# Key-value sums by pairs of tokens in a linear-attention and mixture-of-experts block

## The reference

```
kv = kv + outer(k_t, v_t)          # an 8 x 8 state, from zero in each sequence
ks = ks + k_t
num = q_t @ kv ;  den = q_t . ks + 1e-6
out_t = num / den                  # then out @ W_out + b_out
```

## Time and profile before

| | |
|---|---|
| median of 3 runs | 409.97 us (406.25 to 412.97) |
| the profiled execution | 410.09 us, its span 408.3 us |
| PE busy | 348.2 us, 85% of the span |
| DVE busy | 285.7 us, 70% |
| ACT busy | 264.1 us, 65% |
| POOL busy | 258.4 us, 63% |
| the 32 key-value scans on DVE | 72.9 us |
| the 512 output matmul passes L1302 on PE | 62.8 us |

### The profile page before, as it was taken

One profiled execution on the slowest core, in us unless ns is written; L12 is line 12 of the kernel. 1 busy time (PEld: TensorE's weight loads), 2 busy tenths in 40 slices (PEclk: granted clock), 3 DMA queues, 4 the chain that ended last, 5 costly groups with the idle time before them and its releaser, 6 DMA issues.

```text
span 408.3 us, 8196 instructions
## 1 busy us (share of the span) xinstructions
PE 348.2 (85%) x2523; PEld 299.0 (73%) x2530; DVE 285.7 (70%) x685; ACT 264.1 (65%) x700; POOL 258.4 (63%) x328
## 2 busy tenths in 40 slices
PE   7888498989878999888998839499999998998884
PEld 3447257887766878766787839389989998998863
DVE  4989488998978889987944504176554538777666
ACT  4959266796976859786536733256655558678665
POOL 8786675657849587593885556466654555486650
PEclk9969979999999989999899977789999999999999
DMA  6577455574462504234067325299977869988317
GB/s 201 160 210 199 86 159 112 116 210 118 136 177 70 162 27 141 79 95 127 28 189 228 106 94 171 77 245 259 310 219 226 252 223 350 308 282 244 119 55 206
DMA packets 53521, 69.17 MB, mean 169 GB/s; under 512 B 6365, under 2 KB 37386, under 8 KB 53482
## 3 DMA queue, kind: packets, MB, share of 16 engines
q1 hardware_dynamic: 47556, 58.58, 50.0%
q0 software_dynamic: 4544, 9.35, 6.6%
q10 hardware_dynamic: 1382, 0.79, 0.7%
HBM read 40.06 MB, written 18.15 MB: 143 GB/s over the span
## 4 chain that ended last, share of the span: by engine, by line
PE 35%; ACT 17%; another core or an unknown queue 11%; DVE 10%; issue 8%; POOL 6%; POOLq 1%; DVEq 0%; ACTq 0%
PE bO L1302 6%; PE bS L1523 5%; PE bA L1274 4%; PE bO L1523 4%; ACT hs L1127 3%; ACT L1018 2%; DVE w_lo L2078 2%; ACT shared L899 2%; ACT shared L891 1%; DVE SH L2027 1%; PE bT L1352 1%; POOL KV L705 1%; POOL expert_lists L681 1%; PE bV L1496 1%
## 5 line engine op out<-in xcount | busy, mean ns | idle before, releaser
L797 POOL DMA_INDIRECT expert_results<-yb,yrow x78 | 79.6, 1020 | 62.0 <-DVE yb L2110 35.8
L681 POOL DMA_INDIRECT expert_lists<-rows,pos x64 | 63.1, 985 | 23.0 <-issue 23.0
L1673 DVE TENSOR_TENSOR_SCAN KV<-bS,KV 128x1024 f32<-128x1024 bf16 x32 | 72.9, 2282 | 4.8 <-POOL KV L705 4.5
L1302 PEld LDWEIGHTS bO<-wout_rot,Z 128*128 128x128 f32 x512 | 59.8, 192 | 10.7 <-POOL Z L762 4.6
L1302 PE MATMUL bO<-wout_rot,Z 128*128 128x128 f32 x512 | 62.8, 277 | 5.7 <-POOL Z L762 2.0
L1127 ACT ACTIVATE hs<-bV,KV 128x256 f32<-128x256 f32 x56 | 22.0, 476 | 22.4 <-remote 9.8
L2102 DVE COPY yrow<-xb 128x2 int32<-128x2 int32 x24 | 5.2, 217 | 43.2 <-PE bS L1523 15.4
L1523 PE MATMUL bO<-KV,hs 128*128 128x128 f32 x232 | 30.8, 288 | 1.7 <-ACT hs L1127 1.7
L1274 PE MATMUL bA<-w2s_sb,hs 128*128 128x128 f32 x224 | 30.7, 289 | 0.0
L1523 PEld LDWEIGHTS bO<-KV,hs 128*128 128x128 f32 x232 | 28.8, 201 | 2.6 <-ACT hs L1127 2.5
L1274 PEld LDWEIGHTS bA<-w2s_sb,hs 128*128 128x128 f32 x224 | 28.7, 204 | 0.1
(11 more groups left out here) (371 smaller groups left out, 989.2 us busy)
## 6 DMA issues: line engine op xcount, KB each, us to landing
KV<-packed_weights SPq DMA_DIRECT2D x21, 578.0 KB
Z<-packed_weights SPq DMA_DIRECT2D x18, 578.0 KB
xb<-expert_lists SPq DMA_DIRECT2D x39, 129.0 KB
vr<-vr SPq DMA_DIRECT2D x16, 224.0 KB, 2.5
shared<-expert_results SPq DMA_DIRECT2D x7, 512.0 KB, 6.1
vr<-vr SPq DMA_DIRECT2D x16, 192.0 KB
vr<-vr SPq DMA_DIRECT2D x16, 160.0 KB
vr<-vr SPq DMA_DIRECT2D x16, 128.0 KB
```

Source lines behind the costliest of these rows:

```text
L681: g.indirect_dma_start(out=lists, out_offset=bass.IndirectOffsetOnAxis(ap=pos[:, m:m + 1], axis=0), in_=rows[:, m // TILES, m % TILES, :], ...
L797: g.indirect_dma_start(out=results, out_offset=bass.IndirectOffsetOnAxis(ap=yrow[n][:, c], axis=0), in_=yb[n][:, c, :], in_offset=None).th ...
L1302: ins = t.matmul(bO[:, j * D:(j + 1) * D], Z[:, d, j * P:(j + 1) * P], wout_rot[:, d], start=False, stop=True, skip_group_check=True)
L1673: v.tensor_tensor_scan(w, ps_keep, w, 0.0, ALU.mult, ALU.add).then_inc(s["kv_sum"], 1)
```

## The change

Each sequence is taken as 128 pairs of tokens. VectorE's scan runs over pairs, with state = (even term + state) + odd term, and writes only the odd tokens, so that it has half the elements. It becomes one scan per d and sequence, 128 elements, both operands in SBUF. The array `SUMS` has 257 places per sequence, the first of which stays zero. An even token reads the sum of the odd token ahead of it, which lacks its own term. That term is (q . k of the head) * v: VectorE multiplies q and k of the even tokens, one matmul with a matrix of ones per head (`same_head`) sums over the channels, VectorE multiplies by v and adds the result to Z[:, 0]. Z[:, 0] therefore becomes ready last of the first four, and the output matmuls take d in the order 1, 2, 3, 0, 4, 5, 6, 7. Bank bS is now free for the matmul's result, and the memsets that wrote `keep` there are gone.

```diff
+        same_head = sb("same_head", [P, E, H])
-        KV = sb("KV", [P, E, STEP])
+        SUMS = sb("SUMS", [P, E, STEP // L, L + 1])
+        KV = SUMS[:, :, :, 1:]
+        own = sb("own", [P, STEP // L, L // 2])
+        def sums_at(d):
+            part = SUMS[:, d]
+            return bass.AP(part.tensor, part.offset, [part.ap[0], part.ap[1], [2, L // 2], [2, 2]])
...
-                    g.tensor_tensor(Z[:, 0], KV[:, 0], qn[:], ALU.mult).then_inc(s["z0_ready"], 1)
+                    g.tensor_tensor(by_twos(Z[:, 0]), sums_at(0), by_twos(qn[:]), ALU.mult).then_inc(s["z0_ready"], 1)
...
                 act.wait_ge(s["kv_last"], lasts(st))
+                act.wait_ge(s["own_ready"], st)
                 a.activation(r_qk[:, 1], bB[:], ACT.Relu, bias=bk_col)
...
                 if again:
+                    act.wait_ge(s["own_scaled"], st)
                     act.wait_ge(s["kv_prod"], prods(st, 0))
...
+            def own_sums(st):
+                pe.wait_ge(s["own_ready"], st + 1)
+                t.matmul(bS[:, 0:STEP // 2], same_head[:].rearrange("p e h -> p (e h)"),
+                         own[:].rearrange("p s m -> p (s m)"), start=True, stop=True).then_inc(s["own_summed"], 1)
-                for d in ((0,), (1,), (2, 3), (4, 5), (6,), (7,))[part]:
+                for d in ((1,), (2, 3), (0,), (4, 5), (6,), (7,))[part]:
...
+                if head:
+                    own_sums(i)
                 if nxt:
                     project(i + 1)
...
+            v.tensor_reduce(same_head[:], ident[:].rearrange("p (e h) -> p h e", e=E).unsqueeze(1)
+                            .broadcast_to([P, E, H, E]), AX_X, ALU.add)
-                w = KV[:, 2 * part:2 * part + 2].rearrange("p a t -> p (a t)")
-                v.tensor_tensor_scan(w, ps_keep, w, 0.0, ALU.mult, ALU.add).then_inc(s["kv_sum"], 1)
+                for d in (2 * part, 2 * part + 1):
+                    for q in range(STEP // L):
+                        two = KV[:, d, q].rearrange("p (m o) -> p o m", o=2)
+                        ins = v.tensor_tensor_scan(two[:, 1], two[:, 0], two[:, 1], 0.0, ALU.add, ALU.add)
+                ins.then_inc(s["kv_sum"], 1)
+            def own_terms(i):
+                dve.wait_ge(s["qn_copied"], i + 1)
+                v.tensor_tensor(own[:], evens(seqs(qn[:])), evens(seqs(keys)), ALU.mult).then_inc(s["own_ready"], 1)
+            def own_values(i):
+                dve.wait_ge(s["own_summed"], i + 1)
+                v.tensor_tensor(own[:], ps_own, evens(seqs(vr[:, 0])), ALU.mult).then_inc(s["own_scaled"], 1)
+            def own_added(i):
+                dve.wait_ge(s["own_scaled"], i + 1)
+                dve.wait_ge(s["z0_ready"], i + 1)
+                v.tensor_tensor(evens(seqs(Z[:, 0])), evens(seqs(Z[:, 0])), own[:], ALU.add).then_inc(s["z0_whole"], 1)
-                v.tensor_tensor(Z[:, first:first + n], KV[:, first:first + n],
-                                bK[:].unsqueeze(1).broadcast_to([P, n, STEP]), ALU.mult).then_inc(s["z_ready"], 1)
+                for d in range(2 * part if part > 1 else 3, 2 * part + 2):
+                    ins = v.tensor_tensor(by_twos(Z[:, d]), sums_at(d), by_twos(bK[:]), ALU.mult)
+                ins.then_inc(s["z_ready"], 1)
...
-                    link(v.memset(bS[:], PAIR_OF_ONES))
-                    link(v.memset(bS[:].rearrange("p (s l) -> p s l", l=L // 2)[:, :, 0:1], ZERO_AND_ONE))
...
                     sums(i, 2)
+                    own_terms(i)
                     if routed:
                         route_place(i)
...
                     sums(i, 3)
+                    own_values(i)
+                    own_added(i)
                     zed(i, 1)
```

More of the change, by code:

```diff
@@ L228, in sandwich_kernel @@
         ends = sb("ends", [1, NE], I32)
-        kvz = [w[:].rearrange("p a t -> p (a t)") for w in (KV, Z)]
+        kvz = [SUMS[:].rearrange("p a s t -> p (a s t)"), Z[:].rearrange("p a t -> p (a t)")]
         wb = [kvz[n // 3][:, (n % 3) * WROW:(n % 3 + 1) * WROW] for n in range(NBUF)]
@@ L253, in sandwich_kernel @@
         bE = bV[1]
-        ps_den, ps_keep = bB[:, 0:TILES * H], bS[:].bitcast(BF16)
+        ps_den = bB[:, 0:TILES * H]
+        ps_own = bS[:, 0:STEP // 2].rearrange("p (s m) -> p s m", s=STEP // L)
         def ps_lg(i):
@@ L556, in _ @@
             g.memset(past[:, 0:1], 1.0)
+            g.memset(SUMS[:, :, :, 0:1], 0.0)
             g.memset(ones_seg[:], 1.0).then_inc(s["consts"], 1)
@@ L1167, in _ @@
             act.wait_ge(s["fin_mv"], NS - 1)
-            a.activation(ve[:, 0:3], mv[:, 0:3, :, 1], ACT.Sqrt, bias=ln_eps[:, 0:1]).then_inc(s["fin_root"], 1)
+            a.activation(ve[:, 0:3], mv[:, 0:3, :, 1], ACT.Sqrt, bias=ln_eps[:, 0:1]).then_inc(s["fin_act"], 1)
             act.wait_ge(s["fin_own"], 2)
@@ L1172, in _ @@
             act.wait_ge(s["fin_mv"], NS)
-            a.activation(ve[:, 3], mv[:, 3, :, 1], ACT.Sqrt, bias=ln_eps[:, 0:1]).then_inc(s["fin_root"], 1)
+            a.activation(ve[:, 3], mv[:, 3, :, 1], ACT.Sqrt, bias=ln_eps[:, 0:1]).then_inc(s["fin_act"], 1)
             act.wait_ge(s["fin_own"], 5)
@@ L1678, in zed @@
                     dve.wait_ge(s["qn_copied"], i + 1)
-                first = 2 * part if part > 1 else 3
-                n = 2 * part + 2 - first
-                v.tensor_tensor(Z[:, first:first + n], KV[:, first:first + n],
-                                bK[:].unsqueeze(1).broadcast_to([P, n, STEP]), ALU.mult).then_inc(s["z_ready"], 1)
+                for d in range(2 * part if part > 1 else 3, 2 * part + 2):
+                    ins = v.tensor_tensor(by_twos(Z[:, d]), sums_at(d), by_twos(bK[:]), ALU.mult)
+                ins.then_inc(s["z_ready"], 1)
             def logits_in(i):
@@ L1751, in count @@
                 dve.wait_ge(s["cnt_done"], 1)
-                v.tensor_copy(counts[:], ps_all).then_inc(s["cnt_read"], 1)
+                link(v.tensor_copy(counts[:], ps_all))
             def noted(ins):
@@ L2167, in _ @@
             residual(7, 0, 2)
-            dve.wait_ge(s["fin_half"], 1)
+            dve.wait_ge(s["fin_act"], 3)
             residual(7, 2, 4)
```

72 lines of the change are left out of this document (41 added, 31 removed).

## The result

The changed kernel takes 459.4 us (median of 4, 457.5 to 462.9) where the kernel before took 409.8 in the same runs. The ratio is 1.125, 95% interval 1.114 to 1.136. It is 49.6 us slower: the sign and the mechanism are those of the forecast, the size is 1.8 times the forecast's 27.3, and the time lies above the range (417 to 454). Timed once more beside other kernels it was 48.5 us slower (ratio 1.115, 1.109 to 1.121). Some executions of a kernel are slower by some per cent at a lower granted clock: times, differences and ratios here are of the other executions, but the profiles of four variants (no own term with the scans from PSUM, the own-term matmul last in its second timing, and the two that combine several edits) are of such a slower one.

A forecast was written before the change was run, and what follows sets the result against it. The prediction took the chain of waits up to ACT's writing of the values, not VectorE's scans, as the bound. Steps with the port, 7.0 + 5.4 + 3.3 + 9.2 + 2.4 = 27.3, on 410.1 gave 437 us, range 417 to 454.

The forecast's parts named there:

- What bounds the kernel: Attention steps: VectorE's scans don't set the pace, it idles 1.91 and 1.29 us per iteration; what reaches ACT's value write counts.
- The price of each instruction: On VectorE: four short scans 1.46 us where one took 2.28, an own-term instruction 0.5 us, its Zs costed at nothing.
- The floor: Sum over all attention steps without port contention between VectorE and GpSimd: 12.9 us.
- Steps 0 and 1: First two iterations: own-term matmul delays TensorE's projections, +3.4 and +4.1 us; with the port +7.0 and +5.4.
- Steps 3 to 6: Iterations 3 to 6: quad and multiply after GpSimd's product exceed ACT's slack, +4.4 us; with the port +9.2.
- Step 7: Last iteration: only the last sum's delay, 0.95 us, or +2.4 with the port.
- Step 2: Iteration 2: 0 without the port; with it quads wait for GpSimd's product and Zs before ACT's write, +3.3 us.
- The port doesn't bite: Rival, chance 0.20: 128-element scans slip in between GpSimd's instructions, so only the 12.9 us apply: 423 us.
- Strided reads and turns: Rival, chance 0.20: engines alternate per instruction (+9 us) and strided reads cost VectorE more (+5): 451 us.
- VectorE is the bound: Rival, chance 0.05: VectorE limits the kernel and saves 1.8 us per step, 8 times: 395 us.
- Hidden: Rival, chance 0.07: idle time on the chain absorbs the added waits, time unchanged: 410 us.
- What would show it: Expected signs: some scans over 1 us beside GpSimd, ACT released by VectorE's multiply (iterations 2 to 6), TensorE idle (0 and 1).

The follow-up runs named there:

- both PSUM edits: Changed kernel with the scans' first input and the first own-term multiply's queries read from PSUM, even tokens' terms left out: 391.8 against 375.2 us, ratio 1.041.
- the kernel with the pause: Changed kernel, with GpSimd's first Z of an iteration also waiting for VectorE's first own-term multiply: +36.1 us over before, ratio 1.092; again 447.4 against 413.7 us.

## Why the prediction was wrong in size

**What bounds the kernel** held. VectorE's scans don't set the pace: with all costs of the change taken away, the shorter scans give 0.8%.

**The price of each instruction** held. A quad alone took 1.36 to 1.39 us (1.46 forecast), an own-term instruction 0.39 to 0.43 (0.5), `same_head` 1.87 (1.2 to 2.0), VectorE's Z 0.68. Reads 8 bytes apart cost almost nothing. The Trainium skill's rule in "Vector Engine (DVE) Microarchitecture Reference", Measured stream behaviour on trn2, would have made the Zs dearer by half or more; this case's 680 against 660 ns speaks against using it at a distance of 8 bytes.

**The floor** came near in its sum: 12.9 us, and the kernel in which neither scans nor first multiply have two SBUF inputs is 16.6 us slower than before, with the last own-term instruction still stalling. Part of that is luck. *Steps 0 and 1* were right, without the port (3.4 + 4.1 = 7.5 us; that kernel begins iteration 2's routing at 72.6 us, the one with no own term at 65.8, so 6.8) and with it (forecast 7.0 + 5.4 = 12.4, measured 10.5), since VectorE and GpSimd took turns there, as forecast. But *Steps 3 to 6* of the floor rest on ACT's wait. It is there (1.6 us, forecast 1.3 or 0.5), yet the kernel without it has iterations as long (27.5 us against 27.3), and the order of the output matmuls, which costs 8 to 9 us in all, stands in the floor with 0.95 us in *Step 7* alone.

**The step that failed** is the port's share in *Steps 3 to 6* (+9.2) and with it those of *Step 2* (+3.3) and *Step 7* (+2.4). They rest on the sentence that a quad beside GpSimd "waits for the instruction in hand and then holds GpSimd for 1.46 us". For steps 2 to 7 that made 14.9 us; the iterations lost 42.6. In terms of the port: 27.3 - 12.9 = 14.4 us forecast, about 32 measured. Two things were wrong in it:

- *How long one stall is.* I read the price from one row, 1.78 us at 30.35 beside four Zs, where the engines did take turns. That holds for iterations 0 to 2; from iteration 3 on VectorE stood beside product and Zs for 4.2 to 5.6 us once in each. The old kernel with its mask in SBUF shows both without anything else of the change.
- *Who is caught.* The sum has no wait of TensorE from iteration 3 on: it takes for granted that the quad behind qn is out before the product. In iteration 3 the quad ended at 122.67 instead of 117.64. TensorE idled 35.3 us in all ahead of the own-term matmul, 18.5 of them from iteration 3 on (4.6 to 4.7 us in each but iteration 4), and ACT 36.1 ahead of the values:

```profile
L1329 PE MATMUL bS<-own,same_head 128*128 128x256 f32 x16 | 8.6, 637 | 35.3 <-DVE own L1726 35.3
```

```profile
L977 ACT ACTIVATE vr<-bV,bkv_col 128x512 f32<-128x512 f32 x7 | 4.8, 687 | 36.1 <-PE bV L1268 30.8 <-issue 5.3
```

The margin that I relied on was small: in iteration 3 the quad started 0.55 us ahead of the product and took 6.40 us, in iteration 4 2.2 us ahead, and it took 1.37. But then the last quad was caught, with 5.15 us, and iteration 4 lost 7.0 us where 3 and 5 lost 8.1 and 8.8. Moving the stall to another instruction helped little (the scans from PSUM, the multiply first), and a pause for VectorE gave back 15 us.

**The rivals.** *The port doesn't bite* (423 us) is near what the kernel with both PSUM edits measures: 4% over before, where 423 us is 3%. *Strided reads and turns* (451 us) was closest in time. Its strided price is not there, but its last quad that waits for Z of d = 1 and two routing instructions is what iteration 4 shows, with the next Z as well:

```profile
152.84 5.15 DVE L1720 TENSOR_TENSOR_SCAN SUMS<-SUMS 128x128 f32<-128x128 f32 x4 [1.73 <-POOL SUMS L736]
```

*VectorE is the bound* and *Hidden* have nothing for them.

**What would show it** was right in kind (scans over 1 us where GpSimd works, TensorE idle ahead of the own-term matmul), but I placed TensorE's wait in iterations 0 and 1 only, and ACT's wait was released by TensorE's projection (30.8 of 36.1 us), not by VectorE's multiply. GpSimd's Zs over 1.28 us came where a scan slipped in (1.37 to 1.44).

How the 49 us divide, by subtraction and not by one run: about 32 are stalls by two SBUF inputs, felt mostly through TensorE's and ACT's waits; 8 to 9 the order of the output matmuls; the rest, some 8, the own-term path itself, nearly all in iterations 0 and 1, where its matmul stands ahead of the projections. The parts come from different sets of runs and from kernels that leave out even terms, and they overlap; I estimate each to be good to some 3 us, by what two kernels timed twice differed (2.4 and 2.1 us).

## What to carry to other kernels

In these kernels an instruction of VectorE that reads two operands from SBUF is exposed to GpSimd; one with an operand in PSUM is not. Before trading a long scan with one SBUF input for short ones with two, look at what GpSimd has queued at that time, and cost the stall up to that whole string and not as one instruction (here both came, by iteration), then ask who waits for the instruction that is caught. If GpSimd's work must stand beside such an instruction, a pause ahead of its next long instruction, or halves instead of wholes, can be worth more than the time that they add.

## What the runs showed of the hardware

- VectorE can stand, and GpSimd not, while several of GpSimd's two-input instructions follow one another: a scan of 0.39 us took 5.45 us, GpSimd's product kept 2.35 and its Z 1.26 us. The Trainium skill states in "SBUF — State Buffer", Who interferes with whom, of VectorE's two-port modes, that the one who issues first has the shared ports for the whole instruction and the other blocks. The trace agrees for instructions with two SBUF inputs that one blocks fully; that a blocked one can stay blocked over two to four further instructions is what these traces show (two behind the product in iteration 3 of the changed kernel, four in iteration 4).
- It isn't always so: VectorE got in at the end of the product before 256-element multiplies, and in turn with them (0.88 and 0.81 us); between Zs of 512 elements it got in 69 times of 118, never when it already stood at the Z's start. The cause is open.
- Where both inputs of a long scan lie in SBUF, GpSimd stands as well: a 4-element add took 2.17 us instead of 0.20, and in iteration 0 a Z of 1.26 us took 3.25.
- TensorE's idle time cost twice here. After 4.57 us idle the granted clock was 0.54 over the three projections (the level of 1.2 GHz for most of the stretch), and they went from 124.05 to 129.10, 5.1 us, where before they took 2.7; in the next 7 us it was 1.00.
- The kernel before took 375 us in one set of runs and 410 to 414 in the others. Most of that lies in the expert part: the kernel with the pause started its eighth iteration's routing at 245.7 us in that set and at 251.0 in the other, and took 165 and 190 us from there to the end. Why that part ran faster in one set no run shows. Differences in us carried over between the sets (36.1 and 33.7, 40.8 and 38.7), ratios less so.
